# Where GpSimd gathers batch 0's routed rows in round 14: all eight at the beginning, or three and five behind its root pieces

## The reference

```
xn = layernorm(x)
x  = x + attn0(xn) + moe(xn)
xn = layernorm(x)
x  = x + attn1(xn) + sqrt((xn @ cos(theta'))**2 + (xn @ sin(phi'))**2)

attn0: 16 heads of 8 channels, weights softmax(-sqrt(max(|q|^2 + |k|^2 - 2 q.k, 1e-12)))
attn1: 16 heads of 8 channels, weights softmax over q.k / sqrt(8), row sums applied to the token's own v
moe:   each token goes through a shared SwiGLU of width 352 and through the one of 7 experts
       that its router picks; both results are scaled by factors of the router's probability
```

## Time and profile before

| | |
|---|---|
| time, median of 3 runs | 1465.37 us (1465.34 to 1466.09) |
| time of the profiled execution | 1468.72 us |
| span in the profile | 1467.0 us |
| ScalarE busy | 1428.0 us, 97% |
| VectorE busy | 1220.8 us, 83% |
| TensorE busy | 1110.7 us, 76% |
| GpSimd busy | 884.5 us, 60% |

### The profile page before, as it was taken

How to read it: one execution, slowest core, us unless ns; L and a number is a source line. 1 busy time by engine, 2 the same in 40 slices (tenths; PEclk the granted TensorE clock), 3 DMA queues, 4 the chain that set the end, 5 groups by cost and what they waited for, 6 DMA issues and landing times.

```text
span 1467.0 us, 22437 instructions
## 1 busy us (share of the span) xinstructions
PE 1110.7 (76%) x8231; PEld 445.9 (30%) x8260; DVE 1220.8 (83%) x2196; ACT 1428.0 (97%) x796; POOL 884.5 (60%) x656
## 2 busy tenths in 40 slices
PE   5587787888788888888887675777777677776766
PEld 2133224245143352452542311322223122221212
DVE  6998889978879879789788588838898898998886
ACT  3999999999999999999999999989999999999998
POOL 5188998878789898898898985933213023022100
PEclk8599988999999999899999897889999999999999
DMA  4942544222322235254353231034033033021020
GB/s 121 253 141 65 167 129 125 60 61 73 82 82 62 64 102 155 80 144 131 83 155 96 69 75 31 13 120 81 27 128 71 27 113 81 27 106 33 23 70 20
DMA packets 113185, 130.04 MB, mean 89 GB/s; under 512 B 42906, under 2 KB 81178, under 8 KB 113066
## 3 DMA queue, kind: packets, MB, share of 16 engines
q1 hardware_dynamic: 107738, 116.74, 29.5%
q0 software_dynamic: 4464, 11.09, 2.8%
q10 hardware_dynamic: 864, 0.69, 0.2%
HBM read 83.79 MB, written 44.70 MB: 88 GB/s over the span
## 4 chain that ended last, share of the span: by engine, by line
ACT 38%; POOL 27%; DVE 15%; issue 12%; PE 6%; DMA 2%; SPq 1%; ACTq 0%; DVEq 0%; POOLq 0%
ACT exp L1352 13%; ACT scores L830 11%; ACT scores L791 6%; DVE exp L1360 6%; DVE scores L737 6%; POOL scratch L775 3%; POOL scores L773 3%; ACT exp L1348 3%; PE pvb L718 3%; POOL gate L1098 3%; POOL scratch L784 3%; POOL scores L786 3%; POOL scratch L780 3%; ACT h L1091 2%; POOL scratch L777 1%
## 5 line engine op out<-in xcount | busy, mean ns | idle before, releaser
L737 DVE TENSOR_SCALAR scores<-ring 128x1024 f32<-128x1024 f32 x512 | 591.8, 1216 | 62.2 <-PE ring L703 58.9
L830 ACT ACTIVATE scores<-scores 128x8192 f32<-128x8192 f32 x63 | 438.9, 7020 | 0.2
L1352 ACT ACTIVATE exp<-ring 128x1024 f32<-128x1024 f32 x438 | 431.4, 1388 | 4.4 <-PE ring L1327 3.9
L718 PE MATMUL pvb<-scores,val 128*9 128x256 f32 x4096 | 338.3, 406 | 97.8 <-ACT scores L830 63.7
L1327 PE MATMUL ring<-stk 128*128 128x512 bf16 x995 | 300.9, 386 | 131.2 <-ACT exp L1352 103.4
L791 ACT ACTIVATE scores<-scores 128x7296 f32<-128x7296 f32 (+2 forms) x59 | 384.1, 6574 | 4.9 <-DVE scores L737 4.8
L1360 DVE SCALAR_TENSOR_TENSOR exp<-exp 128x512 f32<-128x512 f32 x438 | 322.3, 758 | 62.6 <-ACT exp L1352 55.6
L703 PE MATMUL ring<-stk 64*128 64x512 bf16 x1024 | 216.1, 419 | 59.2 <-DVE scores L737 45.4
L1327 PEld LDWEIGHTS ring<-stk 128*128 128x128 bf16 x1024 | 66.1, 97 | 341.7 <-ACT exp L1352 232.5
L703 PEld LDWEIGHTS ring<-stk 64*128 64x128 bf16 x1024 | 50.0, 94 | 303.4 <-DVE scores L737 182.3
L718 PEld LDWEIGHTS pvb<-scores,val 128*9 128x9 f32 x4096 | 65.8, 89 | 226.9 <-issue 223.5
(11 more groups left out here) (263 smaller groups left out, 1434.9 us busy)
## 6 DMA issues: line engine op xcount, KB each, us to landing
stk<-stack SPq DMA_DIRECT2D x192, 192.0 KB, 2.8
w<-in_w SPq DMA_DIRECT2D x39, 352.0 KB, 3.6
w<-in_w SPq DMA_DIRECT2D x39, 192.0 KB, 2.7
stack<-qp SPq DMA_DIRECT2D x7, 768.0 KB, 4.4
stack<-kp SPq DMA_DIRECT2D x7, 768.0 KB, 5.4
xj<-xg SPq DMA_DIRECT2D x10, 448.0 KB
yg<-xj POOLq DMA_DIRECT2D x10, 448.0 KB, 3.6
stack<-qp SPq DMA_DIRECT2D x7, 512.0 KB, 5.1
```

The costliest lines, as they stand in the source:

```text
L718: mm = nc.tensor.matmul(pvb[place % 2][32 * c:32 * c + VW, 0:256], val[place][:, j, :], S[place][:, j * N + c * 256:j * N + (c + 1) * 256] ...
L737: nc.vector.tensor_scalar(S[place][:, j * N:(j + 1) * N], tile, 1e-12, None, ALU.max).then_inc(o.release(("qk", group, place, j)), 1)
L830: nc.scalar.activation(S[place][:], S[place][:], ACT.Exp, scale=-1.0).then_inc(exp_done, 1)
L1352: nc.scalar.activation(EX[k // 2][:, k % 2, :], tile, ACT.Exp, scale=SCALE1).then_inc(o.release(("qk1", n, i)), 1)
```

## The change

In round 14 GpSimd no longer issues the eight gathers before its root pieces. It issues three between the pieces of place 1 and place 2, and five between the piece of place 2 and its stores of attention. `pool_gather` gets the bounds for that. In the other batches, in layer 1, nothing changes, and no other engine's program changes.

```diff
-        def pool_gather(pool, b):
+        def pool_gather(pool, b, lo=0, hi=NT):
             if b:
                 pool.wait_ge(k_split1, b)
-            for t in range(b * NT, (b + 1) * NT):
+            for t in range(b * NT + lo, b * NT + hi):
                 pool.indirect_dma_start(
...
                     if r == PLACE_ROUND:
                         pool_place(pool, o, chain)
-                    if r == ADD1_ROUND:
-                        pool.wait_ge(y_stored, Y_ALL)
-                        pool_gather(pool, 0)
...
                     if r > 1 and r != PLACE_ROUND + 1:
                         pool_roots(pool, o, roots, r, 1)
+                    if r == ADD1_ROUND:
+                        pool.wait_ge(y_stored, Y_ALL)
+                        pool_gather(pool, 0, 0, 3)
                     if r == FIRST_JOBS or r > PLACE_ROUND + 1:
                         pool_roots(pool, o, roots, r, 2, 0, 1)
+                    if r == ADD1_ROUND:
+                        pool_gather(pool, 0, 3, NT)
                     if r:
                         pool_store_out(pool, r - 1)
```

## The result

The changed kernel takes 1467.43 us (median of 20 runs, 1465.76 to 1470.02) against 1465.36 us for the kernel before (20 runs on the same chip). The ratio is 1.0017, with a 95% interval from 1.0010 to 1.0024: 2.5 us longer, 1.5 to 3.5. (The means are 2.50 us apart, the medians 2.07.) The profiled execution took 1468.88 us, its span 1467.1 us.

What follows compares the result with a forecast made beforehand. VectorE was taken as pacemaker of round 15, ScalarE as the bound in layer 1. Routed adds 4.9 us later, less 0.4 and 0.65, gave +3.8 with the holes' 3.75 already included: 1469.2 us, range 1466.5 to 1473.0.

Steps and rivals of the forecast that it cites:

- a loss partly swallowed: Rival: faster normalisation or unseen slack before 975.00 removes 1 to 3.3 of the 3.8 us, 1465.9 to 1468.2; chance 0.17.
- same: Whole kernel: time within about 0.2% (2.9 us) of the kernel before; chance 0.26.
- slower: Whole kernel: time more than 0.2% above the kernel before; chance 0.66.
- What the change takes away: Round 14, places 0 and 1: VectorE's two holes go, its work comes 3.75 us earlier, and ScalarE's 3.46 us wait goes.
- What it puts on GpSimd: Round 14, GpSimd: first piece at 849.85, three gathers 3.8 us, five 6.2 us to 888.7, last rows landing at 889.8.
- What lies beside it: Round 14: shared adds beside place 2's piece slow gathers by 0.5 us; routed adds start at 890.3, 4.9 us later.
- The adds push GpSimd back: Rival: VectorE's adds delay place 2's piece by up to 2.2 us, total 6.0 us slower, 1471.4; chance 0.07.
- Holes only under the profiler: Rival: timed runs lack round 14's holes, so the change gains nothing and is 7.3 us slower, 1472.7; chance 0.25.
- From the routed adds to the first scores: Round 14 to layer 1: 4.9 us late, less 0.4 of TensorE wait and 0.65 in round 15, leaves 3.8.
- I find no slack between them and 975.00: Round 15's end to layer 1's first scores: last root and GpSimd's string move by 3.5 to 3.8 us, nothing absorbed.

Runs made afterwards that it cites:

- plain loads: Kernel before, with batch 0's eight gathers replaced by eight plain DMAs of 128 rows at the same place in GpSimd's order: 1461.02 us, ratio 0.9972.
- two unused products: Kernel before, with two TensorE matrix products whose result nothing uses placed ahead of layer 1's first scores: 1465.58 us, ratio 1.0006.

## Why the prediction was right, and what it mis-sized

The forecast was 3.8 us slower (1469.2), the measurement is 2.5 (1467.4): slower, as predicted, and within the whole range. But it is below the forecast's own range of 1468.0 to 1470.6, where I had put the case of a loss partly swallowed. And at 0.17% it is under the 0.2% that I had taken for the border: the case "same", which had 0.26, and not "slower", which had 0.66. The interval excludes no change all the same.

**What the change takes away: right.** VectorE's holes came with the eight gathers: none in three executions of the change, 3.72, 3.75 and 4.22 us in three of before, none with plain loads. ScalarE lost 3.46, 3.47 and 3.45 us to them in the three of before, and nothing after. The shared adds came 4.4 us earlier on average (40.25 against 44.66 us into the round), not 3.75: small waits around the holes went too. The prediction had read VectorE as without idle time behind its second hole; there is one more wait of 0.26 us, at 853.77.

**What it puts on GpSimd: right.** First piece 11.08 us into the round (forecast 11.35), the eighth gather's end at 49.82 (50.2). The three gathers took 3.69 us to the next piece (3.8), the five 6.03 to the stores (6.2).

**What lies beside it: the right total from wrong parts.** I added 0.5 us for gathers slowed by the shared adds. No gather was slowed: five of 0.94 to 0.99 us. But the landing took longer than my 1.15 us: 1.64 us from the last gather's end to the first routed add, and 1.62 and 1.64 in the repetitions. Together 0.5 and 1.15 make the same 1.65.

**The adds push GpSimd back: refuted.** It was the adds that waited, 5.39 us in place of 2.18, and the piece beside them lost nothing (866.11 to 880.45, 14.34 us, the same as before). The same side lost in the other overlaps: normalisation 5.5 to 7.2 us beside a piece and 2.13 without, while that piece takes 8.3 to 8.5 us beside it and 8.3 held back. VectorE, then GpSimd, in the changed kernel:

```profile
876.84 3.75 DVE L1190 SCALAR_TENSOR_TENSOR X<-ysh,WT,X 128x128 f32<-128x128 f32 x2
```

```profile
878.37 2.08 POOL L786 TENSOR_TENSOR scores<-scores,scratch 128x896 f32<-128x896 f32 x1
```

Two of the eight adds carry the whole loss. They took 1.60 and 2.23 us, and the second ended at 880.60, 0.15 us behind the piece's last instruction. The other six took 0.34 to 0.40 us each, although gathers were being issued beside them. The normalisation shows the same pattern: its eight instructions took 0.70 to 1.31 us each, and each ended about 0.08 us behind one of the piece's, which took 0.56 to 1.13 us. The rule of the Trainium skill, "SBUF — State Buffer", Who interferes with whom, is that a VectorE instruction with two inputs in SBUF and a GpSimd instruction that reads SBUF lock each other out for a whole instruction. The trace agrees, with one add to one GpSimd instruction. The normalisation has one tile as its input. The same section of the Trainium skill counts such instructions in as well where their operands let them use both port pairs. The pattern above agrees with that too; no run tries other operands. I had put the stalled adds at up to 4.8 us, hidden by the rows' lateness. They took 5.39, and hidden they were: over at 882.23, 6 us before the rows. The 4.8 came from 2.75 us for the normalisation alone, eight times the median of one instruction. In the rows such instructions overlap by some 0.07 us, and the eight alone take 2.13.

**Holes only under the profiler: refuted.** The two numbers that matched, 3.35 us between the profiled and the timed runs and 3.46 us of hole, had nothing to do with each other. The kernel with plain loads has no holes and gains its 4.1 us in timed runs, which holes in profiled executions alone could not give. The profiled execution of before was just a long one: its span was 1467.0, those of the two repetitions 1463.7 and 1466.0, and 2.07 us of it are the wait ahead of the fourth exponential, which the second execution doesn't have. This rival had 0.25 and should have had less.

**From the routed adds to the first scores: right, with one term too small.** I let the wait for TensorE take 0.4 us off the delay. It was 0.40 in the trace that I had, but 0.93 and 0.95 in the next two, 0.76 on average. The normalisation was 0.4 us longer on average (7.19, 5.53, 5.54 against 6.07, 5.54, 5.52), which I had set equal. Round 15 itself was shorter by 0.82 us (forecast 0.65). So 4.68 - 0.76 + 0.38 - 0.08 (the tile's row overlaps that of the normalisation) = 4.2 at its first tile, 3.4 at its last, and from there I found the slack to be none, as I had said: 3.4 at the first scores.

**The step that was mis-sized: the delay at layer 1's first scores is the end's.** "I find no slack between them and 975.00" holds up to the first scores. Behind them the sum has no term at all. It took the 2.07 us of ScalarE's wait ahead of the fourth exponential as common to both kernels, without looking at it. It is there when TensorE is at half clock at that moment: in two of three executions of before (clock 0.60 and 0.81, waits of 2.07 and 0.80 us) and with plain loads (0.79, 0.78 us), in none of the change. On average this gives back 1.0 of the 3.4 us. That the half clock causes the wait is read from the rows: five products in 2.34 us against 1.24 us, and no such wait in any of the eleven traces at full clock, the one with two unused products among them. That the timed runs have it as often was not shown, and that the order of the gathers decides it wasn't either; so it is open how much of these 1.0 us the change brings and how much was the luck of three executions.

## What to carry to other kernels

Before moving a step to where "the engine is free", write down for the old and the new place what it disturbs and what it delays. Here the old place cost about 4 us through stalls on other engines. The new one removed it and put the routed adds 4.7 us behind where they had been with it. The better answer was between: runs of gathers short enough not to disturb, early enough not to be late, and the GpSimd piece that fell beside VectorE's critical normalisation held back for 2 us. What delays the engine that paces a round should be looked for instruction by instruction beside it, not only in the waits that the profile lists: the slowed adds and the slowed normalisation show no wait at all, only longer instructions. Where an effect is read from one profiled execution, ask what the same kernel looks like in a second one: a wait that comes with the clock of one execution isn't a property of the kernel.

## What the runs showed of the hardware that was not expected

- A run of indirect gathers from GpSimd stalls TensorE, and through it VectorE and ScalarE. VectorE's holes begin 4 to 7 us behind the first gather: 3.1 to 4.8 us for eight in a row, 1.0 and 1.9 us for six, 0.6 us for four at the beginning of the round and none for four behind place 1's piece, none for three. (The change's five fell where VectorE had no distance tile to wait for, and tell nothing.) Eight plain DMAs of the same bytes from the same engine, in 4.38 us, cause none. In the hole of the kernel before it is TensorE that stands still, and the profile has no releaser for it:

```profile
849.21 0.39 PE L703 MATMUL ring<-stk 64*128 64x512 bf16 x2 [1.23 <-issue]
...
850.75 0.90 PE L718 MATMUL pvb<-scores,val 128*9 128x256 f32 x2 [0.61 <-issue]
852.18 0.58 PE L726 MATMUL pvb<-fixed_full,ot 128*128 128x128 f32 x2 [0.53 <-issue]
853.57 0.61 PE L703 MATMUL ring<-stk 64*128 64x512 bf16 x2 [0.80 <-issue]
```

  These waits are 3.2 us together, and none is put down to another engine. In other traces some are put down to VectorE, which itself waits for TensorE (1.69 us with eight gathers behind place 1's piece). What holds TensorE there stays open; it wasn't tried.
- VectorE lost against GpSimd's root pieces in every overlap seen here: L1215, 128 elements a partition, takes 0.27 us alone and 0.7 to 0.9 us beside a piece, and the piece loses at most 0.2 us of 8.3. Each slowed VectorE instruction ends about 0.1 us behind one of GpSimd's. Holding back one piece for 2 us was worth 4.4 us by the timed ratios (1.0017 against 0.9987).
- TensorE's granted clock where layer 1 begins differs between executions of the same kernel: 0.60, 0.81 and 1.00 over seven microseconds. It was below 1.00 in the three of fourteen traces in which TensorE had stood idle longest for the stack load (3.38, 2.83 and 2.64 us), and 1.00 in the others.
